# Moving four weight-slice splits, one residual addition, and VectorE's clip and sum in a one-core decoder layer

## The reference

```
x1 = layernorm(x + attention(x) @ ow + ob)         # 32 heads of 32, softmax over 512 keys
q1 = clip(round(x1 / s1 + z1), 0, 255)             # 1024 x 1024
q2 = clip(round(context / s2 + z2), 0, 255)        # 2 x 1024 x 1024
x2 = layernorm(x1 + ((q1 - z1) * s1) @ ((q2 - z2) * s2))
x3 = layernorm(x2 + x2 @ W_base.T + b_base + low-rank experts, top 2 of 8 by a router)
```

## Time and profile before

| | us |
|---|---|
| median of 3 runs (lowest, highest) | 743.92 (742.16, 744.4) |
| the profiled execution | 742.01 |
| its span, first to last instruction | 740.2 |
| TensorE busy | 713.7 |
| VectorE busy | 467.9 |
| ScalarE busy | 426.2 |
| GpSimd busy | 247.6 |

### The profile page before, as it was taken

The page is one execution under the profiler, slowest core; times in us unless marked ns, Lnnn a source line. Parts: engine busy times, 40 slices in busy tenths (PEclk is TensorE's granted clock), DMA queues, the critical chain, the costliest instruction groups (busy, mean ns, idle before and its releaser), DMA issues.

```text
span 740.2 us, 11755 instructions
## 1 busy us (share of the span) xinstructions
PE 713.7 (96%) x3512; PEld 531.5 (72%) x3512; DVE 467.9 (63%) x831; ACT 426.2 (58%) x919; POOL 247.6 (33%) x189
## 2 busy tenths in 40 slices
PE   6999999999999999999999998998999978999996
PEld 5877768668668677677686685666676756888884
DVE  5886557567467566575575573574775699666464
ACT  5468668568677676686686686654553663311111
POOL 6270240150150060051042069556524464121111
PEclk9999999999999999999999999999999998999999
DMA  8666436335436426436333576638342333122101
GB/s 292 172 191 200 116 84 197 111 84 195 118 82 196 122 72 203 112 81 196 98 99 108 148 213 201 199 92 275 118 142 86 117 141 115 58 88 83 57 30 57
DMA packets 55732, 98.97 MB, mean 134 GB/s; under 512 B 10896, under 2 KB 21392, under 8 KB 54800
## 3 DMA queue, kind: packets, MB, share of 16 engines
q1 hardware_dynamic: 55408, 98.13, 43.7%
q10 hardware_dynamic: 288, 0.39, 0.2%
HBM read 56.41 MB, written 16.65 MB: 99 GB/s over the span
## 4 chain that ended last, share of the span: by engine, by line
PE 68%; issue 13%; POOL 7%; DVE 5%; SPq 3%; DMA 2%; ACT 1%; POOLq 0%; DVEq 0%; ACTq 0%
PE bank L466 42%; PE bank L593 7%; PE bank L607 7%; PE bank L563 7%; PE bank L718 2%; POOL xb L1179 2%; SPq L250 2%; DMA c_raw<-in_ctx 2%; POOL big_lo L1122 1%; PE bank L519 1%; PE bank L692 1%; POOL big_lo L1171 1%; POOL mv L1158 1%; POOL big_hi L1120 1%; DVE st L1432 1%
## 5 line engine op out<-in xcount | busy, mean ns | idle before, releaser
L1358 DVE TENSOR_REDUCE m_col<-bank 128x1 f32<-128x512 f32 x256 | 172.7, 687 | 78.7 <-PE bank L563 78.1
L859 ACT ACTIVATE probs<-bank 128x512 f32<-128x512 f32 x256 | 152.2, 597 | 121.5 <-PE bank L593 118.3
L864 ACT ACTIVATE bank<-bank,m_col 128x512 f32<-128x512 f32 x256 | 169.4, 662 | 18.4 <-DVE m_col L1358 17.4
L466 PE MATMUL bank<-big_hi,w_hi 128*128 128x512 f32 x384 | 157.2, 409 | 5.6 <-DVE big_lo L1255 5.6
L466 PE MATMUL bank<-big_lo,w_hi 128*128 128x512 f32 x384 | 152.8, 398 | 0.0
L466 PE MATMUL bank<-big_hi,w_lo 128*128 128x512 f32 x384 | 151.4, 394 | 0.0
L1109 POOL TENSOR_SCALAR c_raw<-c_raw,sc 128x1024 f32<-128x1024 f32 x16 | 19.2, 1200 | 258.2 <-DMA c_raw<-in_ctx 252.6
L563 PE MATMUL bank<-kp,qp 96*128 96x512 f32 x256 | 101.5, 396 | 1.1 <-ACT bank L864 1.1
L593 PE MATMUL bank<-qp,kp 98*128 98x512 f32 x256 | 101.0, 398 | 0.0
L466 PEld LDWEIGHTS bank<-big_hi,w_hi 128*128 128x128 f32 x384 | 73.4, 191 | 24.6 <-DVE big_lo L1255 6.2
L466 PEld LDWEIGHTS bank<-big_hi,w_lo 128*128 128x128 f32 x384 | 73.1, 190 | 17.2
(11 more groups left out here) (140 smaller groups left out, 1023.6 us busy)
## 6 DMA issues: line engine op xcount, KB each, us to landing
w_raw<-in_wqkv SPq DMA_DIRECT2D x7, 1536.0 KB, 7.7
c_raw<-in_ctx SPq DMA_DIRECT2D x16, 512.0 KB, 4.0
qp<-q_hi SPq DMA_DIRECT2D x128, 64.0 KB, 2.0
kp<-k_hi SPq DMA_DIRECT2D x124, 64.0 KB, 2.0
big_raw<-in_xT SPq DMA_DIRECT2D x16, 256.0 KB, 5.9
qp<-q_lo SPq DMA_DIRECT2D x64, 64.0 KB, 2.0
c_scratch<-c_q SPq DMA_DIRECT2D x16, 256.0 KB, 2.2
r_all<-r_scratch SPq DMA_DIRECT2D x64, 64.0 KB, 2.0
```

The lines of the kernel that those rows point to most:

```text
L466: mm = nc.tensor.matmul(dst, lhs[a], rhs[b], start=(k == 0 and n == 0) if first is None else False, stop=(k == last_k and n == 2))
L859: nc.scalar.activation(probs[:, j, t, :], bank(ST0 + i % 2), ACT.Exp).then_inc(sem["exp_ok"], 1)
L864: nc.scalar.activation(bank(max_bank(s, n)), bank(max_bank(s, n)), ACT.Exp, bias=m_col[:, n:n + 1], accum_out=l_col[:, 1 - par, n:n + 1]). ...
L1358: nc.vector.reduce_max(m_col[:, n:n + 1], bank(max_bank(s, n)), AX, negate=True).then_inc(sem["rowmax"], 1)
```

## The change

Only the order of instructions within the queues of GpSimd and VectorE is changed. On GpSimd the splits of slices 0 to 3 of the left half of the output weight are put in front of the wait for the last context tile in step 15; `residual(1)` is put in front of `split_tile(3)`, `rstd1(1)` in front of `residual(2)`, and `rstd1(2)` in front of `add_correction(0)`. On VectorE `quantise(0)` is put in front of `residual_sum(1)`, and `column_correction(0)` behind `first_mean(2)`, so that `quantise(1)`, `residual_sum(2)` and `first_mean(2)` come ahead of it. `split_ow` itself is as before, defined earlier.

```diff
             def step(s, par, g):
...
                 if proj:
 
+                    if isinstance(s, int) and s == UNITS - 1:
+                        for k in range(KT // 2):
+                            split_ow(0, k)
                     wait_alone(pool, sem["ctxq_in"], 16 * (s + 1))
...
             steps_of(pool, step)
-            for k in range(KT):
+            for k in range(KT // 2, KT):
                 split_ow(0, k)
             split_tile(0)
             split_tile(1)
...
             residual(0)
             rstd1(0)
+            residual(1)
             split_tile(3)
-            residual(1)
+            rstd1(1)
             residual(2)
-            rstd1(1)
             residual(3)
+            rstd1(2)
             add_correction(0)
-            rstd1(2)
             add_correction(1)
...
             dve.wait_ge(sem["sc_ok"], 6)
+            quantise(0)
             residual_sum(1)
-            quantise(0)
             first_mean(1)
             row_correction(0)
-            column_correction(0)
             quantise(1)
             residual_sum(2)
             first_mean(2)
+            column_correction(0)
             split_cx(4)
```

More of the change, by code:

```diff
@@ L1096, in _, with split_ow @@
             pool.wait_ge(sem["plus_ok"], 1)
+            def split_ow(h, k):
+                cols = slice(h * S, (h + 1) * S)
+                pool.wait_ge(big_in[h][k // 4 * 4], 48 - 16 * h)
+                nc.gpsimd.tensor_scalar(big_hi[:, k, cols], big_raw[:, k, cols], 1.0, 0.0, ALU.mult, ALU.add).then_inc(sem["ow_hi"], 1)
+                pool.wait_ge(sem["ow_hi"], h * KT + k + 1)
+                nc.gpsimd.tensor_tensor(big_lo[:, k, cols], big_raw[:, k, cols], big_hi[:, k, cols].bitcast(f32), ALU.subtract).then_inc(sem["ow_lo"], 1)
             def step(s, par, g):
@@ L1114, in step @@
                     split_w(g + 1, 2, 3 * s + 3)
[L1116 to L1122, removed]
             def split_tile(n):
```

## The result

The changed kernel takes 735.61 us (median of 6 runs, 735.07 to 736.66), against 743.04 (741.75 to 744.43, 6 runs) for the kernel before: a ratio of 0.9901, 95% interval 0.9883 to 0.9918. It is faster by 7.4 us. I had forecast 4.9, and the time lies 0.5 us under my range. The 743.92 that the forecast started from is the median of three of these six runs of the kernel before.

The account below looks back on a forecast made before the run. TensorE, busy 713.7 of 740.2 us, was taken as the bound, so only its waits could shrink. Removing 1.97 + 2.91 = 4.88 us from the 743.92 median gave 739.0 us, range 736.1 to 742.0.

Parts of the forecast that it names:

- the two waits: TensorE's waits for context tile 0 near 450 and VectorE's sum of tile 2 near 509: 1.97 and 2.91 us, both forecast gone.
- 4.88: Total saving in us forecast from removing TensorE's two waits, 1.97 + 2.91.
- the tile's wait: TensorE's wait from 450.73 to 452.70 for GpSimd's low half of context tile 0; forecast to go, all 1.97 us.
- the sum's wait: TensorE's wait from 508.76 to 511.67 for VectorE's sum of tile 2; forecast to go, all 2.91 us.
- rival 3: TensorE's half clock from 614 on, 2.7 us lost, may be left out (736.3) or doubled (741.7); chance 0.08.
- Rival 1: One wait stays because something else is late: 739.3 from VectorE-GpSimd collisions, 742.0 or 741.0 with a whole wait; chance 0.12.
- my worst case: Each SBUF instruction of VectorE on the chain comes second to GpSimd, clip of tile 1 until 505.6: stall 0.3, time 739.3.
- Rival 2: Late weight or slow GpSimd delays the last context scale, blocking VectorE's clip and maxima: 744.2 or 746.5; chance 0.05.
- the 0.7 us of room: VectorE's idle time at 436.96; once gone, slices begun after 425.8 cost TensorE us for us.
- Rival 4: The stages behind give the gain back, VectorE being busy 5.29 of 5.50 us there: time 743.9; chance 0.05.
- part 2: Reordered queues of VectorE and GpSimd behind tile 0, claimed to remove TensorE's wait for the sum, 2.91 us.

Follow-up runs that it names:

- The parts alone: Two kernels against the kernel before: only the four weight slices moved early, 740.39 us; only the tail of GpSimd and VectorE reordered, 739.12 us.
- experiment 2: The kernel before with only the tail of GpSimd and VectorE reordered, weight slices left in place: 739.12 us, ratio 0.9956.
- experiment 4: The kernel before run again with nothing changed, for its spread and a second profile: 742.3 us, ratio 1.0004.
- experiment 1: The kernel before with only the four weight slices put ahead of GpSimd's last context scale: 740.39 us, ratio 0.9974.
- experiment 8: The kernel before with the four weight slices moved early and 40 small constant matmuls in the sum's wait: 738.91 us, ratio 0.9957.
- experiment 7: The kernel before with small constant matmuls filling both waits, 24 and 40 of them: 741.52 us, ratio 0.9987.
- experiment 9: The changed kernel with small constant matmuls in TensorE's three waits near 600: 735.58 us, ratio 0.9902 to the kernel before.
- experiment 6: The changed kernel without the moves of residual 1, the inverse deviation of tile 1 and the clip of tile 0: 735.52 us.
- experiment 10: The changed kernel with all eight slices, instead of four, ahead of the last context scale: 742.65 us, ratio 1.0 to the kernel before.
- experiment 5: The changed kernel run again with the whole change, beside the kernel before: 735.58 us, ratio 0.9904.

## Why the prediction was wrong in size

**Right: the two waits and the terms of them.** Both go, and nothing stands in their place. With the 0.6 us put back by which this execution was ahead: first slice 424.4 forecast and 424.4 measured, scale 432.6 and 432.3, tile 0 ready 445.7 and 445.6, first half of tile 2 out at 504.3 and 504.6, transposes 506.8 and 506.5. I left out the overlap behind each wait, so that 4.88 became 5.2 between the profiles; executions of the kernel before at clock 0.994 lie 740.72 - 735.58 = 5.1 above the changed kernel. The parts alone gave 1.8 and 3.1 us.

**Wrong: the step from the profiled execution to the median.** I wrote "The median of the runs is 743.92, 1.9 above it, so I state 743.92 - 4.88 = 739.0", as though what lay between the profiled execution and the median were a fixed amount that the change leaves alone. It was neither fixed nor well measured. The time came out 3.4 us under the 739.0. Of this, 1.7 is the three runs that I took the median of: 743.92 against 742.25 for 62 further executions. Another 0.3 us is the overlap. That leaves about 1.4 us, for which the experiments show half granted clock behind the very waits that the change removes: 1.5 us behind the tile's wait (experiment 2), 1.6 and 1.3 behind the sum's (experiments 4 and 1). The first profile, with clock 0.994, happened to have neither; only 14 of 62 executions have that clock. That profiled execution was also late for another reason, the first 160 us, where 12 of the 13 other profiles were ahead of it by 0.35 to 1.9 us. That the others lost their clock behind these two waits is shown by three profiles and argued for the rest; filling the sum's wait bore it out (experiment 8), filling both in the kernel before gave no clear gain (experiment 7). In the medians the change is worth 6.55 and 7.4 us, not 4.9.

**Wrong: rival 3.** I had the right mechanism in the wrong place. I put the clock's risk at 614, where the trace showed it, at plus or minus 2.7 us. There it is worth nothing (experiment 9, and the same 79.9 to 80.3 us in twelve profiles), because VectorE bounds that stage; rows 11 said so with 5.29 of 5.50 us, and I used that number for another rival. I gave no price to a drop behind the waits at 450 and 509, though waits ahead of a drop were the pattern that I described.

**Rival 1** (a wait that stays) did not come, but its reasoning about VectorE waiting for GpSimd is confirmed three times over: 2.26, 1.59 and 2.43 us for instructions of 0.2 to 0.7. The rule of the Trainium skill ("SBUF — State Buffer", section "Who interferes with whom") agrees with these rows. The collisions ended well before my worst case: the clip of tile 1 at 504.1 with the 0.6 put back, not 505.6. They also show why the clip of tile 0 in front of the sum was of little use: most of what it gained was lost to the collision at the clip of tile 1 (experiment 6).

**Rival 2** was right in its cause and nearly in its size: VectorE 6.8 us late, 6.45 lost (experiment 10). But TensorE stood for 4.7 of it, and the clock, which the rival had not priced, made up most of the rest. Its examples also take off the 0.7 us of room once too often: from a point of 425.8, a start at 431.7 loses 5.9 us, not 5.2.

**Rival 4** did not come: the stages behind handed all of it on.

**A misreading of mine in the experiments:** two clusters 2.4 us apart were six runs of chance. With 62 runs there is one broad spread that goes with the clock, and the profiles show another part of it in the first 160 us.

What stays open: why an execution has the half clock behind a given wait and another has not, and whether one part alone gets its share of the clock back or only both together (experiment 5). The wait before the sum was 2.9 us in both profiles of the kernel before, and only one shows it.

## What to carry to other kernels

Price a removed wait of TensorE at its length and, where TensorE bounds what follows, add what half clock behind it costs in some executions. Before taking the distance between profile and median as fixed, compare the granted clock of the profiled execution with that of the other runs, and don't take the median from three of them: here three were 1.7 us off. A clock drop where another engine is the bound cost nothing here. Filling a wait with idle matmuls can show which case it is, though a single execution is not enough where the drop comes only sometimes. Of a bundle of moves, ask which one ends the wait last: here the correction, with the inverse deviation that it needs, did all the measurable work of part 2.

## What the runs showed of the hardware

- Half granted clock for some us followed waits of TensorE of 2.4 us (experiment 2), 2.9 (experiments 1 and 4) and 4.7 (experiment 10), and did not follow waits of 1.7, 2.0, 2.3 and, in the first profile, 2.9. Behind the first three it cost 1.5, 1.3 and 1.6 us.
- 40 small matmuls of constants (0.06 us each) in the sum's wait kept the clock at full behind it in the profile; the 9 runs had a mean clock of 0.994 and lay within 0.7 us.
- Where VectorE was busy for 4.8 to 4.9 of 5 us (605 to 615), a granted clock of 0.69 and 0.62 or one of 1.00 made no difference to the time (experiment 9).
- An instruction of VectorE that works from SBUF met by one of GpSimd took up to 2.43 us instead of 0.69; the sums that read PSUM took 0.67 to 0.69 us each in all 16 cases of the changed kernel.
